# Another order for the last batch's search of its expert entries, in a cross-attention and mixture-of-experts kernel

## The reference, cut to what matters

```
x = x + tanh(g_xattn) * attention(layernorm(x), ctx)
f = layernorm(x)
scores  = softmax(f @ gate_w.T)
weights, idx = top_k(scores, 2)
y = sum over the 2 chosen e of  weight_e * ((silu(f @ w1[e].T) * (f @ w3[e].T)) @ w2[e].T)
z = (silu(f @ ws1.T) * (f @ ws3.T)) @ ws2.T
x = x + tanh(g_ffn) * (y + z)
```

## Time and profile before

| | us |
|---|---|
| median of 3 runs | 449.25 |
| lowest and highest run | 447.59, 449.43 |
| the profiled execution | 452.13 |
| its span | 450.4 |
| busy in it: TensorE, VectorE, ScalarE, GpSimd | 414.9, 306.4, 239.3, 229.6 |
| the changed stage in it, `router(2, 4)` to the first expert tile | about 234 to 260 |

### The profile page before, as it was taken

The page is one execution under the profiler, slowest core; times in us unless marked ns, Lnnn a source line. Parts: engine busy times, 40 slices in busy tenths (PEclk is TensorE's granted clock), DMA queues, the critical chain, the costliest instruction groups (busy, mean ns, idle before and its releaser), DMA issues.

```text
span 450.4 us, 8467 instructions
## 1 busy us (share of the span) xinstructions
PE 414.9 (92%) x2833; PEld 231.2 (51%) x2834; DVE 306.4 (68%) x663; ACT 239.3 (53%) x432; POOL 229.6 (51%) x206
## 2 busy tenths in 40 slices
PE   7989788999999999998987899999999999999980
PEld 7565445545546554464543455555555555555540
DVE  5989998888688876897869889844444444444430
ACT  2797784676647766855323448734344343434330
POOL 4019435636266762679343217565554646565422
PEclk9999999999999999998998999999999999999997
DMA  8940001706006075084343789575766666666543
GB/s 301 418 169 2 1 12 59 235 3 233 3 1 234 1 262 185 1 304 149 110 143 109 214 285 260 98 138 99 136 106 126 102 130 103 106 126 120 92 62 47
DMA packets 20769, 59.52 MB, mean 132 GB/s; under 512 B 3521, under 2 KB 3521, under 8 KB 20354
## 3 DMA queue, kind: packets, MB, share of 16 engines
q0 software_dynamic: 9504, 20.55, 25.4%
q1 hardware_dynamic: 11234, 38.56, 24.2%
HBM read 35.93 MB, written 23.17 MB: 131 GB/s over the span
## 4 chain that ended last, share of the span: by engine, by line
PE 61%; DVE 19%; POOL 7%; ACT 6%; issue 4%; another core or an unknown queue 1%; DMA 1%; POOLq 0%; DVEq 0%; ACTq 0%
PE bank L1671 46%; PE bank L1676 9%; DVE arena L1062 4%; POOL arena L590 3%; PE bank L1813 3%; POOL GT L615 2%; ACT arena L705 2%; DVE mv L1098 2%; DVE mx L1183 2%; ACT arena L753 1%; DVE xn L1152 1%; POOL ln L557 1%; PE bank L1824 1%; PE bank L1801 1%; DVE arena L1061 1%
## 5 line engine op out<-in xcount | busy, mean ns | idle before, releaser
L1671 PE MATMUL bank<-arena,GT 128*128 x468 | 107.4, 379 | 0.0
L689 POOL DMA_INDIRECT out<-rows,entry x39 | 62.7, 1609 | 65.9 <-issue 33.3
L1671 PE MATMUL bank<-arena,gT 128*128 (+1 forms) x336 | 80.2, 375 | 2.5 <-DVE x_sb L1282 1.3
L1671 PEld LDWEIGHTS bank<-arena,GT 128*128 128x128 f16 x468 | 45.8, 98 | 46.5
L705 ACT ACTIVATE arena<-bank 128x512 f16<-128x512 f32 (+1 forms) x88 | 48.5, 587 | 25.5 <-PE bank L1671 11.4
L666 POOL DMA_INDIRECT rows<-xrows,entry x39 | 38.9, 998 | 33.1 <-DVE entry L1462 11.3
L1062 DVE SCALAR_TENSOR_TENSOR arena<-bank,arena 128x512 f16<-128x512 f32 (+1 forms) x72 | 44.7, 663 | 12.4 <-ACT arena L705 7.5
L1671 PEld LDWEIGHTS bank<-arena,gT 128*128 128x128 f16 x336 | 32.5, 98 | 38.6 <-issue 3.2
L1061 DVE TENSOR_TENSOR gT<-bank,gT 128x256 f16<-128x256 f32 x55 | 23.0, 420 | 42.7 <-ACT gT L705 42.7
L1036 ACT ACTIVATE rows<-bank,weight 128x512 f32<-128x512 f32 x38 | 26.1, 687 | 38.0 <-PE bank L1671 38.0
L1627 DVE SCALAR_TENSOR_TENSOR uu<-th,bank 128x256 f32<-128x256 f32 x39 | 16.4, 421 | 43.4 <-ACT th L1003 42.8
(11 more groups left out here) (177 smaller groups left out, 675.2 us busy)
## 6 DMA issues: line engine op xcount, KB each, us to landing
x_sb<-in_experts SPq DMA_DIRECT2D x9, 768.0 KB, 6.1
rows<-in_experts SPq DMA_DIRECT2D x6, 768.0 KB, 6.3
xrows<-xn SPq DMA_DIRECT2D x16, 256.0 KB
out<-x_sb SPq DMA_DIRECT2D x16, 256.0 KB
image<-GT SPq DMA_DIRECT2D x5, 768.0 KB, 4.2
arena<-image SPq DMA_DIRECT2D x10, 384.0 KB, 4.0
x_sb<-in_x SPq DMA_DIRECT2D x1, 2048.0 KB, 16.8
x_sb<-in_x SPq DMA_DIRECT2D x2, 512.0 KB, 4.0
```

What stands on the lines that cost most here:

```text
L689: nc.gpsimd.indirect_dma_start(out=out, out_offset=bass.IndirectOffsetOnAxis(ap=entry[:, 1, j:j + 1], axis=0), in_=Y[:, j % RING, :], in_o ...
L1671: last = nc.tensor.matmul(dst, a, b, start=n == 0, stop=n == len(steps) - 1)
```

## The change

On VectorE the logits are computed before the two sums of g. The second of these sums and `base(f - 1, 1)` move behind parts of the search. On TensorE `down(f - 1, 2)` and `down(f - 1, 3)` move (the first ahead of `count_pairs`, the second behind `find_entries`), and `turn_g(f, 0)` and `turn_g(f, 1)` one place ahead. On ScalarE the copies of the first two of eight are made before the tanh of `hidden(f, 2)`, and `got0_high` with the first copy of g before the tanh of `hidden(f, 3)`. No instruction is added or removed.

ScalarE's copies of the last batch's rows:

```
-            def send_lists():
+            def send_lists(g0, g1):
                 act.wait_ge(sent_step, 3)
-                for g in range(2 * PER):
+                for g in range(g0, g1):
```

ScalarE, in `last_feed_forward`:

```
                 tanh_h(f, 1)
+                send_lists(0, 2)
                 tanh_h(f, 2)
-                send_lists()
+                send_lists(2, 2 * PER)
+                got0_high()
+                turn_hi(c, "g", 0)
                 tanh_h(f, 3)
-                got0_high()
-                for i in range(PER):
+                for i in range(1, PER):
                     turn_hi(c, "g", i)
```

VectorE, in `last_feed_forward`:

```
+                router_logits(f)
                 turn_lo(f, "g", 2)
-                turn_lo(f, "g", 3)
-                router_logits(f)
                 router_choose(f, 0)
                 router_choose(f, 1)
                 sent_weights()
                 last_place(f)
                 hidden(f, 1)
-                base(f - 1, 1)
                 rows_hot()
                 blocks_hot()
                 pick_tiles()
                 listed_before()
+                turn_lo(f, "g", 3)
                 add_lists()
                 turn_lo(c, "g", 0)
                 read_entries()
                 read_table()
+                base(f - 1, 1)
                 base(f - 1, 2)
```

TensorE, in `last_feed_forward`:

```
                 hidden(f, 1)
+                down(f - 1, 2)
                 count_pairs(f)
                 hidden(f, 2)
-                down(f - 1, 2)
+                turn_g(f, 0)
                 hidden(f, 3)
+                place_lists()
+                turn_g(f, 1)
+                find_entries()
                 down(f - 1, 3)
-                place_lists()
-                turn_g(f, 0)
-                find_entries()
-                turn_g(f, 1)
                 down(f, 0)
```

## The result

| | before | after |
|---|---|---|
| runs, alternating on one chip | 12 | 12 |
| median, us | 449.15 | 451.41 |
| lowest and highest run, us | 447.38, 449.48 | 449.92, 453.47 |
| profiled execution, us | 452.13 | 451.58 |
| its span, us | 450.4 | 449.8 |

The changed kernel takes 1.0065 times the time of the kernel before (95% interval 1.0048 to 1.0083), and its median is 2.26 us higher. (The ratio is not the quotient of the two medians, which is 1.0050: the runs lie in steps, and a median jumps between them.) The median is above the forecast range. It lies at the edge of the class "slower by over 0.5%": just under the 451.5 us that the prediction named for it, with an interval that begins at 1.0048. Yet the two profiled executions differ the other way: after is 0.55 us shorter. Both facts have to be explained together.

A forecast was written before the change was run, and what follows sets the result against it. Expert tiles saturate TensorE from 260 us, so the last batch's search counts by when they begin. Gain 1.64 us, less 0.8 to 1.7 for a clock fall, leaves 0.4: 449.25 - 0.4 = 448.85 us, 448.4 to 449.4; wider range 447.1 to 450.2.

The forecast's parts named there:

- slower by over 0.5%: Whole kernel: a time above 451.5 us, which a measurement can tell from no change; chance 0.03.
- Logits first: VectorE after the router's product: exponential 0.84 us earlier, TensorE's idle time before the count 2.54 to about 0.55 us.
- Copies sooner: ScalarE's 16 copies: four start before the tanh of `hidden(f, 2)`, at 242.40 instead of 245.04 us.
- The entries: End of VectorE's search chain: entries at 249.35 instead of 252.22 us, the search 2.87 us shorter.
- The new wait and the new fall: TensorE behind the entries: about 1.1 us of wait before `down(f-1, 3)`, then a low clock costing 0.8 to 1.7 us.
- the holding clock: Rival for TensorE's new gap: the clock stays up, gain 1.64 us, 447.6 us; chance 0.24.
- my gain: Start of `turn_g(f, 3)` on TensorE: 255.18 instead of 256.82, 1.64 us gained if the clock stays up.
- rival D: Slower: copies and `rows_hot` shorten the search too little; 450.55 us with half the copies' gain; chance 0.11, shared with another rival.
- The gathers stayed hidden: GpSimd's first gather: issued at 250.46, wanted 5.55 us later, at most 5.2 us needed, so no wait on TensorE.

The follow-up runs named there:

- after once more: The changed kernel, unchanged, run and profiled a second time: 453.13 us, ratio 1.005 to the kernel before.
- after, gap filled: The changed kernel plus unread matmuls, three calls behind `place_lists` and four behind `find_entries`: 449.4 us, ratio 0.9979 to the kernel before.
- after, both filled: The changed kernel plus unread matmuls behind `place_lists`, behind `find_entries` and ahead of the last attention product: 449.31 us, ratio 0.9974 to the kernel before.
- moved pair alone: The kernel before with only `base(f-1, 1)` moved behind the table and `down(f-1, 3)` behind `find_entries` and `turn_g(f, 1)`: 451.56 us, ratio 1.0038.
- pair put back: The changed kernel with `base(f - 1, 1)`, the second sum of g and `down(f - 1, 3)` at their old places: 449.55 us, ratio 0.9974 to before.
- pair put back, filled: As pair put back, plus unread matmuls, six calls ahead of the last attention product and four behind `find_entries`: 448.31 us, ratio 0.9969 to before.
- 453.64 us: Profiled execution of the kernel before, unchanged, run once more: 450.66 us in its timed runs, ratio 1.000.
- logits first: The kernel before with only VectorE's `router_logits` moved ahead of its two sums of g: 449.85 us, ratio 0.9983.

## Why the prediction was wrong

Most of the mechanism was as forecast. I take the times from the end of the router's product, since the executions differ before it (it ends at 233.3 to 235.5 us in these, mainly by the clock at 57 and 209 us), to the first expert tile's transposes:

| trace | to the entries | from there to the transposes | together | clock |
|---|---|---|---|---|
| before, profiled at 452.13 us | 17.06 | 5.43 | 22.49 | fell at 240 |
| before, profiled at 448.83 us | 15.56 | 5.37 | 20.93 | full |
| after | 14.35 | 8.16 | 22.51 | fell at 250 |
| after once more | 14.44 | 9.28 | 23.72 | fell at 250, twice as long |
| after, gap filled | 14.45 | 6.54 | 20.99 | full |
| after, both filled | 14.47 | 6.54 | 21.01 | full |
| moved pair alone | 15.12 | 8.22 | 23.34 | fell at 250 |
| pair put back | 14.89 | 5.91 | 20.80 | fell at 251 |
| pair put back, filled | 14.91 | 5.36 | 20.27 | full |

**Logits first.** Right: the wait for the mask went from 2.54 to 0.40 us (0.49 once more), 0.55 forecast, and the full clock stayed. The exponential stood 0.14 us behind ScalarE's two copies once more, where I had put under 0.1.

**Copies sooner.** Right in size, wrong in cause. They started 3.12 us earlier (2.6 forecast), of which 0.57 us are the earlier router. The split cost nothing visible: the tanh at 243.11 stands between copies with no idle time. Had copies and tanh been in different sets of functions, an estimate of up to 5.3 us would have come on top by the Trainium skill, ScalarE: Activation LUTs, section "What ACT_TABLE_LOAD costs", and the trace shows none of it. But only part of the 3.12 us came from the new order: before, the tanh of `hidden(f, 2)` held them because `hidden(f, 2)` had run at the low clock. In the execution at full clock they start 8.80 us behind the router's product, and with the change 7.33.

**The entries.** 2.87 us forecast, 2.71 us measured against the profiled execution of before (17.06 - 14.35), and **1.11 us against the one whose clock stayed up** (15.56 - 14.45).

**The new wait and the new fall.** Right as mechanisms: 1.24 us for `x_sb` (1.1 forecast) and the low clock behind it. Mis-sized: I gave the holding clock a chance of 0.24. All 24 runs of the changed kernel have a mean clock of 0.988 or less, where 45 of 99 of the runs of the kernel before on three chips have 0.990 or more, so I read the fall as one of every run. That is a reading and not shown, since the mean doesn't say where the clock was low. And its price is 8.16 - 6.54 = 1.6 us to 9.28 - 6.54 = 2.7 us, where I had 0.8 to 1.7.

**The step that failed** is "All sums are made in the profiled execution, 452.13 us with a span of 450.4 us. The median of the runs is 449.25 us, and I subtract the same microseconds from it." That execution was 2.7 us slower than the slowest run shown. It held a fall of the clock at 240 us, and the removal of this fall, 1.42 us and what hung on it, is about all of the gain that I counted. The unchanged kernel alone, from that execution to the one at full clock, gives 22.49 - 20.93 = 1.56 us, and my gain was 1.64 us. In an execution that doesn't have it, the search is shorter by 1.11 us only, and 6.54 - 5.37 = 1.17 us go to the wait and to `down(f - 1, 3)` behind the entries: nothing is gained. Then the new fall adds 1.6 to 2.7 us. The prediction noted the spread of the runs as "about what one fall of the clock more or less is worth", and did not ask which of these levels the profile belonged to. By its own rule for rival D (the change breaks even with entries 1.2 us earlier at full clock, 2.9 us with the fall), the 1.11 us give 0.1 us lost at full clock and 1.8 us with the fall. Measured in the medians were 2.26 us. So D's arithmetic was right, and its condition came true by another way than the one I named: not because the copies gained less than their rows said, but because the rows were those of an execution in which the clock had fallen.

The parts can be told apart at full clock. All of the change but the moved pair gains 20.93 - 20.27 = 0.66 us, and the moved pair gives 21.01 - 20.27 = 0.74 us back. The pair also makes a fall at this place dear. With the pair at its old place the fall cost 20.80 - 20.27 = 0.53 us up to the transposes, and 0.3 us more behind them (193.04 instead of 192.75 us to the end). In the changed order it cost 1.6 and 2.7 us. These are single traces. How often the clock falls there with the pair at its old place is open. In the moved pair alone two of the 12 runs (449.40 and 449.57 us) have a mean clock of 0.994, and are 0.75 us slower than the fastest of the kernel before (448.65 us), which fits a price of that order without a fall.

The rest of the difference, from 1.8 to 2.26 us, may be the longer form of the fall. How often it comes is open: one of two traces of the changed kernel has it. The runs of both kernels lie in steps of some 1.6 us, with the mean clock falling along. I read them as one fall more or less, which the traces at 448.83 us (none before 430 us), 452.13 us and 453.64 us (two and three) bear out. In the runs without a trace the falls are not counted.

The gathers stayed hidden: TensorE had no wait for the first one (issued at 250.06, its transposes from 257.10).

## What to carry to other kernels

Before microseconds of a profiled execution are subtracted from a median, compare that execution's time and its low clocks with the timed runs: a fall that the profile shows may be missing in many of them, and a fix for it is then worth little. Work that fills a wait of TensorE at one place opens a gap where it stood, and where nothing behind that gap can be made up for, it costs its idle time and the clock behind it. Multiplications that nobody reads can hold the clock in such a gap, here for 0.7 to 0.9% of the changed kernel's time, if they fit into the idle time (1.14 us of 1.24) and don't stand right ahead of a short product on which another engine waits.

## What the runs showed of the hardware

- The same idle time of TensorE has no fixed consequence. Before the count the clock fell behind 2.54 and 2.51 us (two traces of the kernel before) and behind 1.87 us (logits first), and stayed up behind 2.50 us (the kernel before) and 2.53 us (the moved pair alone). The 1.83 us before the attention product at 209 us ended with the low clock in seven traces and with the full one in three. The 1.73 us before the one at 57 us ended with the low clock in three traces of 13. The wait for `x_sb` of 0.96 to 0.97 us left the clock up in five traces and ended with the low one in the moved pair alone, and the wait of 1.24 us ended with the low one in all three traces without fillers in it.
- In the three traces with the fall before the count the clock had also fallen at 209 us, and in the two without it had not. Five traces are too few to call that a link.
- Two executions of one program with the same gap had 3.4 and 6.6 us at half the clock behind it.
- ScalarE's stall of 3.76 us before its two copies of g, whose releaser the traces don't name, is missing in one trace alone, the first of after. What it waits for stays open, and so does whether it belongs to a chip. Where it is, TensorE also stands 0.37 to 0.55 us in the middle of the router's product, put down to no engine (0.41 in the earlier trace rows), and both go on within 0.05 us of each other (234.92 and 234.96 in the earlier trace rows). That suggests one event for both, which no trace names.
- Sixteen instructions of unused products ahead of the count delayed the count's result by 0.86 us beyond what TensorE's own rows show. I have no row that explains it.
